# A graph network on one core: tiles of the joined stage in a fixed order, with short and empty ones between whole ones

## The reference

```python
k = typed_linear(x, ntype, Wk).reshape(n, H, HS)     # H = 8 heads, HS = 16; q and v likewise
kT = jnp.einsum('nhd,htdo->nhto', k, Watt)           # vT likewise with Wmsg: 32 relations
kw = kT[src, :, etype]
m = vT[src, :, etype]
a = jnp.einsum('ehd,ehd->eh', kw, q[dst]) * pri[:, etype].T / SQRT_D
att = edge_softmax(a, dst, n)
msg = (m * att[:, :, None]).reshape(-1, H * HS)
hag = jax.ops.segment_sum(msg, dst, num_segments=n)
h = jax.nn.silu(typed_linear(hag, ntype, Wa))
alpha = jax.nn.sigmoid(skip[ntype])[:, None]
h = h * alpha + x * (1.0 - alpha)                    # then a layer norm over the 128 values
```

## Time and profile before

| | |
|---|---|
| median of 3 runs | 4191.42 us |
| the profiled execution | 4193.7 us, of which the span is 4191.9 us |
| PE busy | 2356.6 us (56%) |
| DVE busy | 2714.6 us (65%) |
| ACT busy | 1704.9 us (41%) |
| POOL busy | 2537.3 us (61%) |
| DMA queue of POOL | 651.37 MB, 44.0% of 16 engines |
| mean rate of DMA | 187 GB/s |

### The profile page before, as it was taken

The page is one execution under the profiler, slowest core; times in us unless marked ns, Lnnn a source line. Parts: engine busy times, 40 slices in busy tenths (PEclk is TensorE's granted clock), DMA queues, the critical chain, the costliest instruction groups (busy, mean ns, idle before and its releaser), DMA issues.

```text
span 4191.9 us, 54366 instructions
## 1 busy us (share of the span) xinstructions
PE 2356.6 (56%) x12695; PEld 1692.8 (40%) x12786; DVE 2714.6 (65%) x6706; ACT 1704.9 (41%) x3970; POOL 2537.3 (61%) x2596
## 2 busy tenths in 40 slices
PE   3777771455555555555677777245555554555355
PEld 1333331444444444445333333144444444444343
DVE  6666662566666666667688887256666666666465
ACT  3676660223223332324566666023233333323255
POOL 4666556666666666661566664666666666666426
PEclk8899885677777777777799998567777777777666
DMA  8999984344444444444799997434444444444131
GB/s 198 412 409 409 417 355 135 112 125 119 121 116 119 117 120 117 113 117 106 235 392 375 408 399 327 134 110 119 113 112 114 113 114 111 118 115 112 51 111 48
DMA packets 321826, 782.64 MB, mean 187 GB/s; under 512 B 87083, under 2 KB 249803, under 8 KB 309007
## 3 DMA queue, kind: packets, MB, share of 16 engines
q0 software_dynamic: 110672, 651.37, 44.0%
q1 hardware_dynamic: 202387, 127.10, 11.5%
q10 hardware_dynamic: 8448, 0.53, 0.1%
HBM read 335.58 MB, written 573.46 MB: 217 GB/s over the span
## 4 chain that ended last, share of the span: by engine, by line
DVE 17%; another core or an unknown queue 14%; issue 11%; DMA 8%; PE 6%; DVEq 4%; POOL 3%; ACT 1%; SPq 0%; POOLq 0%; ACTq 0%
DMA relation_table<-region,scatter_node 7%; DVE sums L1791 5%; PE bank L1291 2%; DVE region L1754 2%; DVEq L1780 2%; PE bank L1123 1%; DVEq L1791 1%; PE bank L1278 1%; DVE region L1776 1%; DVE region_q L1762 1%; POOL region_q L709 1%; DVE region L1580 1%; ACT region L885 1%; DVEq L403 1%
## 5 line engine op out<-in xcount | busy, mean ns | idle before, releaser
L802 POOL DMA_INDIRECT region<-relation_table,key_of x1664 | 1630.7, 980 | 899.9 <-issue 467.5
L1291 PE MATMUL bank<-region,arena 128*128 128x136 f32 x3328 | 657.1, 356 | 366.0 <-issue 136.5
L1021 ACT ACTIVATE arena<-iota_free,minus_dst 128x128 f32<-128x128 f32 x1664 | 527.9, 387 | 714.9 <-remote 555.1
L885 ACT COPY region<-bank 128x512 f32<-128x512 f32 x1152 | 625.4, 601 | 356.4 <-DMA relation_table<-region,scatter_node 217.5
L1278 PE MATMUL bank<-region_q 128*128 x3328 | 589.5, 328 | 313.1 <-issue 225.2
L1123 PE MATMUL bank<-sums,arena 128*128 128x512 bf16 x1958 | 609.0, 418 | 257.2 <-ACT region L885 178.0
L1580 DVE COPY region<-bank 128x512 f32<-128x512 f32 x896 | 585.0, 685 | 260.1 <-DMA relation_table<-region,scatter_node 165.9
L1291 PEld LDWEIGHTS bank<-region,arena 128*128 128x128 f32 x3328 | 564.3, 248 | 457.5 <-issue 286.0
L1278 PEld LDWEIGHTS bank<-region_q 128*128 128x128 f32 x3328 | 540.3, 242 | 319.6 <-issue 318.4
L1791 DVE TENSOR_TENSOR sums<-sums,bank 128x136 f32 x1664 | 474.0, 285 | 281.8 <-remote 181.0
L1032 ACT ACTIVATE region<-arena 128x256 f32<-128x256 f32 x52 | 21.7, 417 | 1162.0 <-DVE arena L1860 982.7
(11 more groups left out here) (243 smaller groups left out, 2949.5 us busy)
## 6 DMA issues: line engine op xcount, KB each, us to landing
arena<-edge_places SPq DMA_DIRECT2D x416, 128.0 KB
region<-relation_table,key_of POOLq DMA_INDIRECT x1664
arena<-segment_flags SPq DMA_DIRECT2D x104, 128.0 KB
region_q<-q_rows SPq DMA_DIRECT2D x6, 768.0 KB, 6.4
aggregated_rows<-one_less_alpha SPq DMA_DIRECT2D x17, 256.0 KB
region<-aggregated_rows SPq DMA_DIRECT2D x16, 272.0 KB, 3.0
sums<-relation_weight_parts SPq DMA_DIRECT2D x32, 128.0 KB
x_sorted<-arena SPq DMA_DIRECT2D x16, 256.0 KB
```

The costliest lines, as they stand in the source:

```text
L802: pool.indirect_dma_start(out=rows[:, block_.r, q * QUAD + s], out_offset=None, in_=table, in_offset=bass.IndirectOffsetOnAxis(ap=key_of[: ...
L885: nc.scalar.copy(stage[:, r, :, k * HS:(k + 1) * HS], bank[TABLE_BANK + k % TABLE_BANKS][:, :].rearrange("p (t o) -> p t o", t=RT)).then_i ...
L1021: chain.step(nc.scalar.activation(onehots[:, at, s], iota_free[:, :], ACT.Abs, bias=minus_dst[:, bass.ds(block_.b * BLOCK + (q * QUAD + s) ...
L1291: ins = nc.tensor.matmul(bank[SUM_BANK[q % 2][pair]][:, s * SUMC:(s + 1) * SUMC], onehots[:, at, 2 * pair + s], rows[:, block_.r, slot, RH ...
```

## The change

Whole and short tiles are told apart. Each type's whole tiles are numbered through from 0; the rest of each type goes to tile 48 + type (`FULL` = 48). So tiles 0 to 47 are whole or empty, tiles 48 to 63 hold the rests. The 64 tiles are then worked through in a fixed order in spans of eight: places 0, 1, 2, 4 and 6 take the tiles 0 to 39 in turn, place 5 takes one of the tiles 40 to 47, places 3 and 7 take the rests of two types. With the counts above there are 43 whole tiles, so place 5 is whole in the first three spans and empty in the last five. `tile_at` is the tile number at each place; `turn_of` is the place of each node's tile, worked out by arithmetic for `place_row`.

```diff
+FULL, SPAN = NTILES - 1, 8
+NEVER_EMPTY = 5 * SORTED_TILES // SPAN
...
+            by_span = tile_at.rearrange("p (u s) -> p u s", s=SPAN)
+            fives = iota_free[:, 0:NEVER_EMPTY].rearrange("p (u f) -> p u f", f=5)
+            v.tensor_copy(by_span[:, :, 0:3], fives[:, :, 0:3])
+            v.tensor_copy(by_span[:, :, 4:SPAN:2], fives[:, :, 3:5])
+            v.tensor_copy(by_span[:, :, 5:6], iota_free[:, NEVER_EMPTY:FULL].unsqueeze(2))
+            v.tensor_copy(by_span[:, :, 3:SPAN:4], iota_free[:, FULL:SORTED_TILES].rearrange("p (u k) -> p u k", k=2))
+            v.tensor_scalar(last_of, iota_free[:, FULL:SORTED_TILES], float(P), None, ALU.mult)
             dve.wait_ge(type_in, 32)
...
-            link(v.tensor_scalar(tot, bank[1][:, 0:NT], 127.0, None, ALU.add))
-            link(v.tensor_copy(tot_i, tot))
+            link(v.tensor_copy(tot_i, bank[1][:, 0:NT]))
             link(v.tensor_single_scalar(tot_i, tot_i, 7, ALU.logical_shift_right))
             link(v.tensor_copy(tiles_t, tot_i))
             link(v.tensor_tensor_scan(first_tile, ones[:, 0:NT], tiles_t, 0.0, ALU.mult, ALU.add))
+            link(v.tensor_scalar(full_end, first_tile, float(P), None, ALU.mult))
+            chain.step(v.tensor_tensor(last_of, last_of, full_end, ALU.subtract))
             link(v.tensor_tensor(first_tile, first_tile, tiles_t, ALU.subtract))
             link(v.scalar_tensor_tensor(base_t, first_tile, float(P), bank[0][:, 0:NT], ALU.mult, ALU.add))
             link(v.tensor_tensor(ranks, ranks, bc(base_t, 2, NTILES), ALU.add))
+            link(v.tensor_tensor(keep, ranks, bc(full_end, 2, NTILES), ALU.is_gt))
+            link(v.tensor_tensor(keep, keep, bc(last_of, 2, NTILES), ALU.mult))
+            link(v.tensor_tensor(ranks, ranks, keep, ALU.add))
             link(v.tensor_tensor(ranks, ranks, onehot_t, ALU.mult))
...
-            link(v.scalar_tensor_tensor(pos, tile_of_node, float(P), part_of_node, ALU.mult, ALU.add))
-            v.tensor_copy(place_row[:, :], pos)
...
-            tiles_free = bc(iota_free[:, 0:SORTED_TILES], 1, NTILES)
+            tiles_free = bc(tile_at, 1, NTILES)
...
             scale_relations(0)
+
+            link(v.tensor_scalar(span_i, tile_of_node, 205.0, None, ALU.mult))
+            link(v.tensor_single_scalar(span_i, span_i, 10, ALU.logical_shift_right))
+            link(v.tensor_copy(span_no, span_i))
+            link(v.scalar_tensor_tensor(turn_of, span_no, -5.0, tile_of_node, ALU.mult, ALU.add))
...
+            link(v.scalar_tensor_tensor(pos, turn_of, float(P), part_of_node, ALU.mult, ALU.add))
+            v.tensor_copy(place_row[:, :], pos)
             dve.wait_ge(nodes_psum, 1)
...
             left_of_first(0)
-            link(v.tensor_tensor(type_cmp, bc(iota_free[:, 0:SORTED_TILES], 2, NT), bc(first_tile, 1, SORTED_TILES), ALU.is_ge))
+            link(v.tensor_tensor(type_cmp, bc(tile_at, 2, NT), bc(first_tile, 1, SORTED_TILES), ALU.is_ge))
             link(v.tensor_reduce(type_f, type_cmp, AX.X, ALU.add))
             link(v.tensor_scalar(type_of_tile[:, :], type_f, -1.0, None, ALU.add))
+            link(v.tensor_copy(type_of_tile[:, 3:SORTED_TILES:4], type_no[:, :]))
```

More of the change, by code:

```diff
@@ L347, in gnn_kernel @@
         zeros = pb[:, 4608:4608 + 3 * D]
+        tile_at = pb[:, 7936:7936 + SORTED_TILES]
+        full_end = pb[:, 8000:8000 + NT]
+        last_of = pb[:, 8016:8016 + NT]
+        span_no = pb[:, 3296:3296 + NTILES]
+        span_i = pb[:, 3345:3345 + NTILES].bitcast(I32)
+        turn_of = pb[:, 3394:3394 + NTILES]
+        later_at = pb[:, 8032:8032 + NTILES]
         part_of_node = pb[:, 7400:7400 + NTILES]
@@ L1484, in _ @@
             scale_relations(0)
+            link(v.tensor_scalar(span_i, tile_of_node, 205.0, None, ALU.mult))
+            link(v.tensor_single_scalar(span_i, span_i, 10, ALU.logical_shift_right))
+            link(v.tensor_copy(span_no, span_i))
+            link(v.scalar_tensor_tensor(turn_of, span_no, -5.0, tile_of_node, ALU.mult, ALU.add))
+            link(v.tensor_scalar(turn_of, turn_of, -2.0, 0.0, ALU.add, ALU.max))
+            link(v.scalar_tensor_tensor(turn_of, span_no, 3.0, turn_of, ALU.mult, ALU.add))
+            link(v.tensor_tensor(turn_of, turn_of, tile_of_node, ALU.add))
+            link(v.scalar_tensor_tensor(later_at, tile_of_node, 8.0, turn_of, ALU.mult, ALU.subtract))
+            link(v.tensor_scalar(later_at, later_at, float(5 - 8 * NEVER_EMPTY), None, ALU.add))
+            link(v.scalar_tensor_tensor(later_at, tile_of_node, float(NEVER_EMPTY), later_at, ALU.is_ge, ALU.mult))
+            link(v.tensor_tensor(turn_of, turn_of, later_at, ALU.add))
+            link(v.tensor_scalar(later_at, tile_of_node, -4.0, float(8 * NEVER_EMPTY - 4 * FULL - 2), ALU.mult, ALU.add))
+            link(v.scalar_tensor_tensor(later_at, tile_of_node, float(FULL), later_at, ALU.is_ge, ALU.mult))
+            link(v.tensor_tensor(turn_of, turn_of, later_at, ALU.add))
+            link(v.scalar_tensor_tensor(pos, turn_of, float(P), part_of_node, ALU.mult, ALU.add))
+            v.tensor_copy(place_row[:, :], pos)
             dve.wait_ge(nodes_psum, 1)
```

## The result

The median after is 4209.42 us (4205.1 to 4211.26), that of the runs of the kernel before beside it 4193.54 us (4189.73 to 4199.29), seven runs each. The ratio is 1.0034, with a 95% interval of 1.0024 to 1.0044: slower by about 14 us. The profiled execution's span is 4207.6 us, before 4191.9, so **+15.7**.

A forecast was written before the change was run, and what follows sets the result against it. The joined stages were taken as DMA-bound (engines 96% busy mid-stage). Preparation 4.5, first stage 4, q 3, second stage 1.5, q 3 and close 0.5 make +16.5 on the median 4191.42: 4208 us, range 4180 to 4232.

The forecast's parts named there:

- The mechanism of the dry time: Joined stages: empty and short tiles between whole ones let the DMA queue run dry, +28 us first layer, +26 second.
- The signs named for it: Around empty tiles: stores 6 to 7 us apart, DMA share near 0.2 for 4 to 6 us, copies waiting for a landing.
- the prediction's rule: Joined stages: store at the later of previous store + 6.6 us and landing three tiles back + 9.1; dry start 3.4.
- The net of the first stage: First joined stage: 28 us more dry time less 24.1 us got back at its end, +4 (-4 to +8).
- The q loads: End of each joined stage: q row loads now start beside queued stores, +3 us per layer (-1 to +8).
- The second stage: Second layer's joined stage: 26 us more dry time less 24.7 got back, +1.5 (-10 to +8), and q again +3.
- The preparation: Before the first table matmul: added DVE operations delay it by +4.5 us (+2 to +5.3).
- The close: Last group's four scatters: three now store 64 KB or nearly where they stored nothing, +0.5 us (0 to +1).
- the ring rides through: Rival for the joined stages: queue keeps a whole tile in hand across each empty one, -38 us, 4154; chance 0.17.
- tile 6: Whole tile behind a span's empty tile 5: riding through needs 19.1 us to be no more than the 12.5 left.
- Nothing measurable: Rival: other traffic fills dry time to the low ends, full queues hide the preparation; +3.5 us, 4195; chance 0.23.
- Every term at its upper end: Rival: preparation, both joined stages, q loads and close all cost their upper ends; +38 us, 4230; chance 0.18.

The follow-up runs named there:

- e2: Kernel after with the five empty tiles put last again, short tiles spread as in the change: 3724.45 us, ratio 1.0030 to the kernel before.
- e1: Kernel before with as much extra preparation work as the change adds, old tile order: 3718.86 us against 3712.91, ratio 1.0019.
- a0: Kernel after run again without edit, on the chip with the shorter loops: 3724.87 us against 3712.91 for the kernel before, ratio 1.0032.
- a2: Kernel after run once more without edit, on the chip with the shorter loops: 3724.99 us against 3712.95 for the kernel before, ratio 1.0032.
- e5b: Kernel after with the second layer's gathers of the sums issued one per step instead of four at once: 4161.66 us against 4160.15 before, ratio 1.0000.
- e3: Kernel after with SP loading the q rows only once the table's stores have landed: 3722.86 us, ratio 1.0021 to the kernel before.
- e4b: Kernel before with the second layer's gathers of the sums issued one per step instead of four at once: 4151.86 us against 4160.15, ratio 0.9976.
- b1: Kernel before run again without edit, on a third chip: 4163.54 us in one run.
- e8: e4b with each table store issued one step earlier, ahead of the queries' scatter and the gather: 3771.95 us against 3712.95 before, ratio 1.0156.
- e6: Kernel after reordered (two whole tiles, one short or empty, 21 times), places worked out behind the preparation's chain: 3716.42 us against 3712.95 before, ratio 1.0009.
- e7b: e6 with the gathers of the sums also issued one per step: 4150.35 us against 4160.15 for the kernel before, ratio 0.9973.

## Why the prediction was right, and where its terms were off

**The mechanism of the dry time: shown, and its size near.** The forecast was 28 us more of dry time in stage 1; the share gives 25 (0.99 to 0.94 of 500 us). The signs named for it are there: stores 4.7 to 8 us apart in the pairs, share at 0.08 and 0.12 for four us, the empty tile held by a landing. For the second layer 26 was forecast and 25 read. e2 shows both halves of the exchange by undoing them together. It gives some 20 of the 25 back (0.94 to 0.98); the prediction's rule had put all of it down to the empty tiles.

**The net of the first stage: +4 forecast, +5 to +9 found.** Against e1, which has the same preparation, the four profiles of the change (after, a0, a2 and e5b, whose edit is in the second layer alone) are 5.2 to 9.0 us longer, 6.9 in the mean. The exchange of the empty tiles is 2 to 5 of that (e2's 558.3 against 560.0 to 563.8). The rest, some 3.5, is e2 against e1: the even places of the short tiles, as far as one profile of each can tell. The prediction carried those through its rule, but said of a single short tile "old and new alike". The term was near, its parts were not: a share of 0.98 against 0.99 is a loss that the rule of landings and stores doesn't hold.

**The q loads: +3 twice forecast, about 0 found.** This was the weakest step. Held back by the load, the gather comes at most some 1.5 us later (e3). What does come later is the first product, 13.1 us behind the first gather instead of 8.2. It is made up within the loop: from first gather to last sum the change is 2.6 and 1.9 us shorter, not longer, and e1 and a0 differ by 0.4. The prediction had the argument for a low value in hand ("the loop also needed q before") and gave it too little weight. Its price of +8 was a wrong working of a right rule. The Trainium skill (DMA: Bandwidth & Descriptors, "Queues, rings and completion order") has each DMA engine take turns between its queues packet by packet, and this trace agrees: 76 packets of one queue beside 76 of the other. The prediction took turns for equal bytes. With 512 bytes against 32 KB in a turn, the store gives up next to nothing and the load stands until the stores are done.

**The second stage: +4.5 with q forecast, about +3 found.** The profiles give +1 to +5.5 (582.7, 580.1 and 581.3 against 579.2 and 577.1), the first pair +3.5 less 1.9 in the loop, and e1's 581.2 says that it may be nothing at all. e4b and e5b confirm that the late stores cost time, but not their price: take the four gathers apart and the new order's stage falls by 14 us, the old one's by 4 to 6. The rule had late stores cost either order over 20 us of dry time (34 to 37 against 13, 67 to 70 against 45). Without them it puts the new order behind, as in the first layer; the runs have it 5.6 us ahead. So the net of this stage was near while two of its parts were off, and that is luck.

**The preparation: +4.5 forecast, +5 to +6 found.** The front part came out at +2.05 to the hundredth, POOL's gathers followed it (+2.5), and the node numbers came 4.8 us later where 5 was forecast (50.17 against 45.40). The split's last cast then moved by 5.2 (56.37 against 51.20 before) and the first table matmul by 6.1, so the busy queues hid none of it: the upper end, 5.3, was the better value. The first store moved by 5.9 in the first pair and by about 5 in the mean of the runs.

**The close: +0.5 forecast, +2.4 found.** From the last sum to the first scatter of the output and on to the last one, the change needs 2 us more in the first pair (169.9 against 167.5 from last sum to last scatter; 169.6 in e5b against 167.2 in e4b and 168.9 in b1). On the chip with the shorter loops the two orders overlap: 177.2 and 179.3 in e1 and e8, 179.9 and 179.2 in a0 and a2. So the term lies between nothing and 2.4. The tail behind the last scatter is 10.5 us in both. No experiment changed the close alone.

**The sum.** +16.5 was put together from +4.5, +7, +4.5 and +0.5; the profile has +5.9, +5.8 (8.4 - 2.6), +1.6 (3.5 - 1.9) and +2.4, which is 15.7. That 4208 stands so near 4209 is in part luck: q was some 10 us too high with what the loops gave back, and the preparation, the two joined stages and the close together were some 10 too low. On the chip of a0 and a2 the same change costs 12.0, which is 4.5 less than the sum.

**The rivals.** That the ring rides through fell at the point which the prediction named: the queue was dry in front of tile 6. The Trainium skill (Trainium Kernel Development and Optimization, "Best Practices") advises more than one buffer so that DMA and compute overlap. With the three buffers of this kernel they overlap, but not wholly: the DMA share is 0.94 in the change, and the stage didn't come down to the larger of the two loads. "Nothing measurable" needed the preparation hidden; e1 alone costs 0.19% and excludes that. "Every term at its upper end" had the preparation and the first stage right and fell with q.

## What to carry to other kernels

A ring of buffers rides over a cheap item only when the time from a landing to the refilled buffer's store, plus one spacing, plus the start of a dry queue, is no more than the time of the data still queued; dry time moved from the end of a stage into its middle is an exchange, and has to be counted on both sides. An item that moves nothing still takes its turn in the ring. Before a transfer on another queue is priced, compare the sizes of the packets, not the bytes in all: with turns of one packet each, the queue with the small packets stands. And an order worked out on the chip has a price ahead of everything: here 15 small linked operations and three wide ones cost as much as the order itself, so look for a form of the computation that stands behind the first work, as in e6.

## What the runs showed of the hardware that was not expected

- Two queues took turns packet by packet (76 and 76 in 6 us), and with packets of 512 bytes against 32 KB the load all but stood: 0.04 MB beside 2.49. The first two loads of a layer on SP's queue, 768 KB each, took 18.9 to 21.7 us from issue to landing behind two such stores, and 4.6 to 6.5 when none was queued; the stores lost at most some 1.5 us. Where the order ends on more bytes, in e7b (whole, whole, short, whole, against whole, empty, whole, short), it was 25.9 to 28.2.
- SP itself was held: one of its issues of these loads took 14.8 us, against 2.6 at most in the kernel before.
- A gather behind a 4 MB store on the same queue kept its reader waiting 10 us in the mean and 14.6 at most (e8). Issued in small portions ahead of the store, its reader waited 33.0 us in a whole stage (e4b), and in one lump of four it held up the stores instead.
- Three chips of the same kind took 1341, 1324 and 1119 us for the attention loop of the first layer, with the first joined stage alike within some 2 us (old order) to 4 (new). The cause wasn't looked into.
- An exchange of some 20 us of DMA time inside a stage moved the whole by less than 1 (e2 against the change): a share that falls from 0.99 to 0.94 is no measure of a loss by itself.
